# Cross-attention queries by Strassen's scheme, in half groups of four heads

## The chip, the cores and the metric

One core of one Trainium2 chip runs the whole program. The metric is the device time of one execution in microseconds (us), smaller is better. TensorE multiplies matrices (PE in the profile, PEld for its weight loads), VectorE (DVE), ScalarE (ACT) and GpSimd (POOL) work on elements, and SyncE (SP) issues the DMA transfers.

## The reference, cut to what matters

One decoder layer in float32: self-attention, cross-attention, feed-forward. The change is in the cross-attention. Its latents are the normalised x (8 batches, 128 rows, 512 features):

```python
q = (latents @ Wq).reshape(b, q_len, N_KV_HEADS, N_GROUPS, HEAD_DIM)   # 32 heads of 128
k = (hidden_states @ Wk).reshape(b, kv_len, N_KV_HEADS, HEAD_DIM)      # 4 heads, 256 keys
v = (hidden_states @ Wv).reshape(b, kv_len, N_KV_HEADS, HEAD_DIM)
scores = jnp.einsum('bqhgd,bkhd->bhgqk', q, k) * scale
attn = jax.nn.softmax(scores.astype(jnp.float32), axis=-1).astype(q.dtype)
out = jnp.einsum('bhgqk,bkhd->bqhgd', attn, v)
return out.reshape(b, q_len, N_HEADS * HEAD_DIM) @ Wo
```

## The kernel before, in words

Every float32 operand is kept as a rounded high part and a low part that holds the rest (names with h and l). ScalarE writes the high part, VectorE or GpSimd the low part, and each product is three matmuls: high by high, high by low, low by high (split3, lines 222 to 224). So each unit of matrix work costs three matmuls on TensorE.

The latents stand transposed in XTh and XTl: four blocks of 128 features (kc) by 1024 columns, 128 of them for each batch. The 32 query heads are taken in four groups of eight that share a key head. A group is 32 steps; step k treats two heads of one batch. On TensorE a step has these blocks, in this order:

- S: the scores of step k + 2 (scores_b), 6 matmuls of 256 columns;
- V: in every even step, probabilities times values of the last four heads (outputs), 6 matmuls of 512 columns;
- T: four transposes of the probabilities of step k;
- O: a quarter of the output product of the batch before (out_piece, two heads), 6 matmuls of 512 columns, summed in bank 7 over the eight heads of the group, then added to x_res by VectorE (residual);
- Q: half of a query block (queries, one head by half of the batches), 6 matmuls of 512 columns; a block takes 12 matmuls in bank 6 over two steps. There are 64 blocks: 8 ahead of the first step and 56 in the steps, to step 15 of the last group.

Beside it, VectorE takes the maxima of S, ScalarE the exponentials, VectorE the reciprocals of the sums and GpSimd multiplies (norm), two steps ahead of T. After T, ScalarE writes PTh and VectorE PTl; V waits for them. Weights come through four raw slots: SP loads a slot when GpSimd has taken the low part of what was in it. Keys and values of a batch (KV, 512 KB) have three slots, each refilled when the V blocks of the batch in it are done; the next batch is loaded two batches ahead, 32 loads in all. SP does all this in the order of its program: a load whose wait isn't met holds up those behind it.

The order of work on each engine is written out by hand, with semaphores between the engines. After the last group come the expert product, the last O and V blocks, and the feed-forward part in four rounds (pair).

Of the kernel before, what the change touches and what calls it, by code (L numbers as in the profile page):

```python
# [33 lines left out]
P = 128  # L34
# [13 lines left out]
XG = XH // XKV  # L48
KEYS = 2 * P
# [14 lines left out]
def decoder_layer(nc, x, ctx, s_wq, s_wk, s_wv, s_wo, x_wq, x_wk, x_wv, x_wo, gate_w, up_w, down_w,  # L64
                  fc1_w, fc2_w, expert_w, gamma, beta, rope, out):
    with ExitStack() as stack:
# [96 lines left out]
        WOh = sb("WOh", "WO", 0, [XG, D], F32R)  # L163
        WOl = sb("WOl", "WO", 16, [XG, D], F32R)


        Qh = sb("Qh", "Q", 0, [4, 2, 4, P], F32R)
        Ql = sb("Ql", "Q", 16, [4, 2, 4, P], F32R)
        Oh = sb("Oh", "O", 0, [2, XG, P], F32R)
        Ol = sb("Ol", "O", 8, [2, XG, P], F32R)  # L170
# [22 lines left out]
        EXTh = sb("EXTh", "KV", 8, [LC, LAT], F32R)  # L193
        EXTl = sb("EXTl", "KV", 10, [LC, LAT], F32R)
# [60 lines left out]

        ld_ex, c_a_e, c_v_e = sem("ld_ex"), sem("c_a_e"), sem("c_v_e")
# [13 lines left out]
        WPG = 2 * XG  # L270
# [17 lines left out]
        def chunk_steps(last):  # L288

            steps = [((0, 0, 1, 2, 3, 4, 5, 5)[h], "wo", h) for h in range(XG)]  # L290
            if not last:
                steps += [(8 + 2 * h, "wq", h) for h in range(XG)]
            else:
                steps += [(6 + 2 * i, "ffn", i) for i in range(NUP)]
                steps += [(22 + i - NUP, "ffn", i) for i in range(NUP, NUP + NFC)]
                steps += [((17, 19, 21, 26, 27, 28, 29, 30)[c], "ffn", NUP + NFC + c) for c in range(IC)]
            return sorted(steps, key=lambda step: step[0])
# [8 lines left out]
        def targets(kind, i):  # L306
            if kind == "wo":
                return WOh[:, i, :], WOl[:, i, :]
            if kind == "wq":
                return WQh[:, i, :, :], WQl[:, i, :, :]  # L310
            return ffn_chunks[i][1:]
# [4 lines left out]
        def ffn_ready(i):  # L316

            order = [n for n, (_, kind, j) in enumerate(chunk_steps(True)) if kind == "ffn" and j == i]
            return W0 + WPG * (XKV - 1) + order[0] + 1

# [4 lines left out]
        def query_cells(t, head, half):  # L325

            i, h = head // 2, head % 2
            return t[:, :, h, i, :] if half else t[:, i, h, :, :]

        def query_cell(t, head, b):  # L330
            i, h = head // 2, head % 2
            return t[:, b % HALF, h, i, :] if b // HALF else t[:, i, h, b % HALF, :]
        LN3_STEPS = (8, 12)
        EX_STEP = 26
# [30 lines left out]
        def _(sp):  # L365
# [48 lines left out]
            for b in range(3):  # L414
                sp.dma_start(f32(KV[:, b, :]), kv_scratch[0, b]).then_inc(b_kv[b], 16)
# [12 lines left out]
            def first_loads(g):  # L428

                for n in range(4):  # L430
                    src = wo_src(g, n)
                    sp.wait_ge(b_g_w, W0 + WPG * g + n - 3)
                    sp.dma_start(raw[:, n, :], src).then_inc(b_ld[n], 16)

            first_loads(0)
# [4 lines left out]
            def group(g, last):  # L440
                kv_loads = [(4 * (b - 3) + 4, g, b) for b in range(3, NB)]
                if not last:
                    kv_loads += [(24, g + 1, 2), (28, g + 1, 0), (32, g + 1, 1)]
                w_loads = [(max(step - 2, 0), kind, i) for step, kind, i in chunk_steps(last)]
                for k in range(DUOS):
                    for n, (step, kind, i) in enumerate(w_loads):
                        if step == k and n >= 4:

                            sp.wait_ge(b_g_w, W0 + WPG * g + n - 3)
# [39 lines left out]
        def _(gp):  # L489
# [83 lines left out]
            def norm(g, k):  # L573
                gp.wait_ge(b_v_rec, DUOS * g + k + 1)
# [33 lines left out]
            for g in range(XKV):  # L608
                group(g, g == XKV - 1)
# [1225 lines left out]
```

## Time and profile before

| | |
|---|---|
| median of 3 runs | 1024.8 us (1023.59 to 1025.76) |
| the profiled execution, own time | 1024.6 us |
| its span, first to last instruction | 1022.9 us |
| PE, PEld busy | 99%, 83% |
| DVE, ACT, POOL busy | 59%, 51%, 38% |
| granted TensorE clock, mean | 1.000 |
| DMA, mean | 67 GB/s |

Busy shares are of the span. Matmuls overlap in the pipeline, so the mean duration of a matmul is longer than the distance from one to the next; what a block costs is read as the distance between the starts of two blocks in the timeline.

### The profile page before, as it was taken

The numbers are of one execution on the slowest core, as the hardware profiler recorded it, in microseconds if no ns is written. First come the engines' busy times: TensorE is split into PE (matmuls) and PEld (weight loads), VectorE is DVE, ScalarE is ACT, GpSimd is POOL, SyncE is SP. The second block draws the span as 40 slices with busy tenths as digits, with TensorE's granted clock in tenths as the row PEclk, the third lists the DMA queues.
The fourth block names the chain that finished last, engine by engine and source line by source line (L and its number), as shares of the span: only waits on it lengthen the run. The fifth ranks groups of instructions, "written<-read, shape, count | busy, mean of one in ns | idle before, by whom it ended". The sixth has DMA issues, their size and how long they took to land.

```text
span 1022.9 us, 15694 instructions
## 1 busy us (share of the span) xinstructions
PE 1012.8 (99%) x5624; PEld 850.4 (83%) x5624; DVE 603.5 (59%) x1176; ACT 522.6 (51%) x1591; POOL 387.9 (38%) x369
## 2 busy tenths in 40 slices
PE   8999999999999999999999999999999999999997
PEld 7777777777888888888888888888888888899996
DVE  6888888878434545454545445444545556545654
ACT  5766667666524655445545445545436457522211
POOL 3645544544142533324433324333226447412110
PEclk9999999999999999999999999999999999999999
DMA  9410111104552221111211203112112133100000
GB/s 329 126 38 18 29 42 42 42 21 141 169 153 72 65 83 43 63 51 53 83 42 54 82 21 93 42 42 72 63 41 84 42 102 98 29 21 21 21 21 21
DMA packets 70248, 68.38 MB, mean 67 GB/s; under 512 B 4000, under 2 KB 54176, under 8 KB 70176
## 3 DMA queue, kind: packets, MB, share of 16 engines
q1 hardware_dynamic: 70176, 67.43, 21.3%
q8 instruction: 43, 0.70, 0.3%
q14 instruction: 29, 0.24, 0.1%
HBM read 48.55 MB, written 18.87 MB: 66 GB/s over the span
## 4 chain that ended last, share of the span: by engine, by line
PE 94%; DVE 2%; DMA 1%; ACT 1%; issue 1%; SPq 1%; POOL 0%; DVEq 0%; POOLq 0%
PE bank L222 27%; PE bank L224 26%; PE bank L223 26%; PE bank L1019 5%; PE bank L759 3%; PE bank L721 1%; PE bank L725 1%; DMA rawO<-in_L_attn_Wo_dram 1%; PE bank L728 1%; PE bank L731 1%; DVE Kbdl L1482 0%; PE bank L674 0%; PE bank L934 0%; PE bank L686 0%; PE bank L667 0%
## 5 line engine op out<-in xcount | busy, mean ns | idle before, releaser
L576 POOL TENSOR_TENSOR Pb<-Pb,b_rec 128x512 f32<-128x512 f32 x128 | 133.8, 1046 | 346.3 <-DVE b_rec L1634 346.3
L1629 DVE TENSOR_REDUCE b_nb<-bank 128x2 f32<-128x512 f32 x128 | 87.9, 687 | 85.6 <-PE bank L224 85.5
L1119 ACT ACTIVATE PTh<-bank 128x512 fp32r<-128x512 f32 x128 | 76.3, 596 | 117.3 <-PE bank L1019 117.3
L1262 ACT ACTIVATE Pb<-bank,b_nb 128x256 f32<-128x256 f32 x256 | 119.0, 477 | 4.5 <-DVE b_nb L1629 4.5
L1176 ACT ACTIVATE Pa<-bank,a_nb 128x128 f32<-128x128 f32 x256 | 90.8, 369 | 45.5 <-DVE a_nb L1507 44.8
L222 PE MATMUL bank<-WOh,Oh 128*128 128x512 f32 x256 | 110.6, 432 | 0.2
L538 POOL TENSOR_TENSOR Pa<-Pa,a_rec 128x512 f32<-128x512 f32 x64 | 68.3, 1067 | 102.0 <-DVE a_rec L1513 101.4
L1383 DVE TENSOR_TENSOR PTl<-bank,PTh 128x512 fp32r<-128x512 f32 x128 | 87.9, 687 | 25.4 <-ACT PTh L1119 25.4
L222 PE MATMUL bank<-XTh,WQh 128*128 128x512 f32 x256 | 101.6, 397 | 0.0
L224 PE MATMUL bank<-WOh,Ol 128*128 128x512 f32 x256 | 100.9, 394 | 0.0
L223 PE MATMUL bank<-WOl,Oh 128*128 128x512 f32 x256 | 100.4, 392 | 0.0
L224 PE MATMUL bank<-XTh,WQl 128*128 128x512 f32 x256 | 100.0, 390 | 0.0
L223 PE MATMUL bank<-XTl,WQh 128*128 128x512 f32 x256 | 99.7, 390 | 0.0
L1638 DVE SCALAR_TENSOR_TENSOR Ql<-bank,Qh 128x512 fp32r<-128x512 f32 x64 | 44.2, 692 | 80.4 <-ACT Qh L1269 80.4
L1119 ACT ACTIVATE Oh<-bank 128x512 fp32r<-128x512 f32 x64 | 38.3, 599 | 88.8 <-PE bank L224 88.8
L1383 DVE TENSOR_TENSOR Ol<-bank,Oh 128x512 fp32r<-128x512 f32 x64 | 44.3, 692 | 59.9 <-ACT Oh L1119 59.9
L1019 PE MATMUL bank<-ident,Pb 128*128 128x128 f32 x512 | 76.8, 272 | 0.0
L224 PE MATMUL bank<-KV,Ql 128*128 128x256 f32 x256 | 72.4, 283 | 0.0
L223 PE MATMUL bank<-KV,Qh 128*128 128x256 f32 x256 | 72.3, 283 | 0.0
L1269 ACT ACTIVATE Qh<-bank 128x512 fp32r<-128x512 f32 x64 | 38.3, 600 | 66.5 <-PE bank L224 66.5
L222 PE MATMUL bank<-KV,Qh 128*128 128x256 f32 x256 | 71.9, 281 | 0.0
L1019 PEld LDWEIGHTS bank<-ident,Pb 128*128 128x128 f32 x512 | 61.3, 140 | 8.4
(230 smaller groups left out, 2648.4 us busy)
## 6 DMA issues: line engine op xcount, KB each, us to landing
kv_scratch<-KVst SPq DMA_DIRECT2D x64, 256.0 KB, 3.0
KV<-kv_scratch SPq DMA_DIRECT2D x32, 512.0 KB, 3.4
raw<-in_L_xattn_Wo_dram SPq DMA_DIRECT2D x32, 256.0 KB, 3.4
raw<-in_L_xattn_Wq_dram SPq DMA_DIRECT2D x24, 256.0 KB, 4.2
cx<-in_ctx_dram SPq DMA_DIRECT2D x8, 256.0 KB, 9.9
raw_first<-in_L_xattn_Wq_dram SPq DMA_DIRECT2D x8, 256.0 KB, 4.5
raw<-in_L_ffn_up_w_dram SPq DMA_DIRECT2D x8, 256.0 KB, 4.0
raw<-in_L_ffn_down_w_dram SPq DMA_DIRECT2D x8, 256.0 KB, 2.8
```

Of the source, the lines that this page charges most:

```text
L222: pe.matmul(dst, lh, rh, start=start, stop=False)
L223: pe.matmul(dst, lh, rl, start=False, stop=False)
L224: return pe.matmul(dst, ll, rh, start=False, stop=stop)
L538: gp.tensor_tensor(pj, pj, a_rec[:, SG * j:SG * j + SG].unsqueeze(2).to_broadcast([P, SG, P]), ALU.mult).then_inc(g_norm, 1)
L576: gp.tensor_tensor(pk, pk, b_rec[:, k % 4, :].unsqueeze(2).to_broadcast([P, 2, KEYS]), ALU.mult).then_inc(b_g_norm, 1)
L1019: op = pe.transpose(bank[3 + k % 2][:, c * KEYS + h * P:c * KEYS + (h + 1) * P], Pb[:, k % 4, h, c * P:(c + 1) * P], ident[:])
L1119: return act.activation(dst, src, ACT.Copy)
L1176: op = act.activation(Pa[:, j % PS, c * P:(c + 1) * P], bank[2 + j % 3][:, c * P:(c + 1) * P], ACT.Exp, bias=a_nb[:, h:h + 1], scale=1.0, ...
L1262: op = act.activation(Pb[:, k % 4, h, :], bank[k % 3][:, h * KEYS:(h + 1) * KEYS], ACT.Exp, bias=b_nb[:, k % 4, h:h + 1], scale=1.0, accum ...
L1383: return dve.tensor_tensor(dst, src, f32(hi_part), ALU.subtract)
L1629: dve.tensor_reduce(b_nb[:, k % 4, :], bank[k % 3][:].rearrange("p (h k) -> p h k", h=2), AX.X, ALU.max, negate=True).then_inc(b_v_nb, 1)
L1638: dve.scalar_tensor_tensor(out=query_cells(Ql, head, half), in0=bank[bk][:].rearrange("p (b n) -> p b n", b=HALF), scalar=X_SCALE, in1=f32 ...
```

## The change

The groups become half groups of four heads (HG): eight units u of 16 steps (PER), 64 visits v to a batch of two steps each (VISITS), 128 steps in one loop (STEPS), as many as before. S, V, T and O keep their number and size. What differs:

- Query blocks of units 0 and 1 are made as before (8 ahead of the first step, 8 in steps 0 to 15). The other 48 come in 12 groups n of four blocks: two heads by both halves of the batches. Each group is a 2 by 2 product of blocks, made by Strassen's scheme in the Winograd form with seven products of half the depth. Product p of group n is made in step 16 + 8n + p; the eighth step of each group has no Q block. A product is 2 kc by 3, 6 matmuls of 512 columns, so 42 matmuls take the place of 48.
- The left operands of the products (OPh, OPl) are made of two raw weight chunks, 6 steps ahead: four sums on GpSimd of 256 elements a partition (operand_sums), seven high parts on ScalarE (operand_hi) and seven low parts on GpSimd (operand_lo).
- The right operands need sums of latents T1 to T4, made once in steps 2 to 16: eight sums, each two GpSimd instructions and one on VectorE, then high and low part.
- After products 0, 1 and 2 ScalarE copies the running sum in bank 6 to U (partial), and the next product is added on in the same bank. Product 3 completes a block as before. After products 4, 5 and 6 VectorE adds the bank to a U (query_sum), ScalarE writes the high part (query_hi) and GpSimd the low part (query_lo).
- bank 7 is summed over four heads, so x_res is added to 64 times (residual), not 32. The output weights have six places (WOS).
- Keys and values are loaded for each visit, 64 times 512 KB, into three slots. The load for visit v waits for the V block of visit v - 3 (in step 2v - 4), and S needs it at the start of step 2v - 2. In each step of SP it is issued ahead of the weight chunks.
- At the end TensorE runs the expert product, the last V, two O blocks, the transposes of turn_x3, and the last two O blocks.

```diff
-DUOS = NB * XG // 2
-PB = XG // 2
-QUADS = DUOS // 2
-BLOCK = NB // 2 * PB
-QB = PB // 2
+GROUPS = XH // HG
+VISITS = GROUPS * NB
+STEPS = 2 * VISITS
+PER = 2 * NB
...
+        OPh = sb("OPh", "WQ", 0, [7, 2, P], F32R)
...
+        S1 = sb("S1", "WQ", 7, [2 * P])
+        S2 = sb("S2", "WQ", 23, [2 * P])
+        U = [sb("U1", "WQ", 12, [D]), sb("U2", "WQ", 14, [D]), sb("U3", "WQ", 28, [D])]
+        T1h = sb("T1h", "O", 8, [2, D], F32R)
...
+        T2h = sb("T2h", "WO", 24, [2, D], F32R)
...
+        T4h = sb("T4h", "WQ", 8, [2, D], F32R)
...
+        Tf = sb("Tf", "F", 0, [2, D])
+        Qh = sb("Qh", "Q", 0, [2, 2, 2, 2, 2, P], F32R)
...
+        UNIT0, UNITS_Q, PRODUCTS = PER, 2 * (GROUPS - 2), 7
...
+        CHUNKS = [((0, 0, 1, 2)[h], "wo", (0, h), h) for h in range(HG)]
+        CHUNKS += [((PER * (u - 1) + 7, PER * (u - 1) + 10, PER * u + 3, PER * u + 3)[h], "wo", (u, h), 2 + h % 2)
+                   for u in range(1, GROUPS) for h in range(HG)]
+        CHUNKS += [(step, "ffn", i, slot) for i, (step, slot) in enumerate(UP_STEPS + FC_STEPS + DN_STEPS)]
...
+        PAIRS = [(8 * n + 10, "pair", n, slot) for n in range(UNITS_Q) for slot in range(2)]
...
+        def chunk_load_step(step, kind, i, slot):
+            if kind == "pair":
+                return 8 * i + 6 if i else 2
+            ahead = chunk_ahead(kind, i, slot)
+            if ahead and ahead[1] == "pair":
+                return max(step - 3, ahead[0] + 5)
+            return max(step - 3, ahead[0] + 1 if ahead else 0)
...
+        SUMS = ((0, 0, 0), (1, 1, 2), (0, 1, 1))
+        B = [[(XTh[:, 2 * k:2 * k + 2, c * D:(c + 1) * D], XTl[:, 2 * k:2 * k + 2, c * D:(c + 1) * D])
+              for c in range(2)] for k in range(2)]
+        T1, T2, T3, T4 = (T1h, T1l), (T2h, T2l), B[0][1], (T4h, T4l)
+        LATENT_SUMS = [(dst, a, b, kc) for dst, a, b in ((T1, B[0][1], B[0][0]), (T2, B[1][1], T1),
+                                                         (T4, B[1][0], T2), (T3, B[1][1], B[0][1]))
+                       for kc in range(2)]
+        T_STEPS = (2, 3, 5, 6, 8, 9, 13, 14)
+        T_SPLIT = (4, 5, 7, 8, 10, 11, 15, 16)
+        RIGHT = (B[0][0], T2, T3, T4, B[1][0], T1, B[1][1])
...
+        def pair_step(k):
+            return [(n, k - 8 * n - 10) for n in range(UNITS_Q) if 0 <= k - 8 * n - 10 < PRODUCTS]
+        def product_step(k):
+            n, p = (k - UNIT0) // 8, (k - UNIT0) % 8
+            return (n, p) if 0 <= n < UNITS_Q and p < PRODUCTS else (None, None)
+        def products(n, p):
+            return BLOCKS + PRODUCTS * n + p + 1
...
+            def load_chunk(kind, i, slot):
+                ahead = chunk_ahead(kind, i, slot)
+                if ahead and ahead[1] == "pair":
+                    sp.wait_ge(b_g_s, PRODUCTS * ahead[2] + 5)
+                elif ahead:
+                    sp.wait_ge(b_g_w, split_count(*ahead[1:3]))
+                if kind == "pair":
...
+                    src = wq_src(u // 2, HG * (u % 2) + head + slot)
...
+                else:
+                    src = wo_src(i[0] // 2, HG * (i[0] % 2) + i[1]) if kind == "wo" else ffn_chunks[i][0]
+                    dst = raw_view(slot, targets(kind, i)[0])
+                sp.dma_start(dst, src).then_inc(b_ld[slot], 16)
+            for h in range(HG):
+                load_chunk("wo", (0, h), h)
             for n in range(U_E0 + 2, NU):
                 store_unit(n)
             stored(NU)
-            def group(g, last):
-                kv_loads = [(4 * (b - 3) + 4, g, b) for b in range(3, NB)]
-                if not last:
-                    kv_loads += [(24, g + 1, 2), (28, g + 1, 0), (32, g + 1, 1)]
-                w_loads = [(max(step - 2, 0), kind, i) for step, kind, i in chunk_steps(last)]
-                for k in range(DUOS):
-                    for n, (step, kind, i) in enumerate(w_loads):
-                        if step == k and n >= 4:
-                            sp.wait_ge(b_g_w, W0 + WPG * g + n - 3)
-                            dst = targets(kind, i)[0]
-                            src = (wo_src(g, i) if kind == "wo" else wq_src(g + 1, i) if kind == "wq"
-                                   else ffn_chunks[i][0])
-                            sp.dma_start(raw_view(n % 4, dst), src).then_inc(b_ld[n % 4], 16)
-                    if k == 26 and not last:
-                        first_loads(g + 1)
-                    for done, gg, b in kv_loads:
-                        if done == k + 1:
-                            sp.wait_ge(b_pe_pv, QUADS * g + done // 2)
-                            sp.dma_start(f32(KV[:, b % 3, :]), kv_scratch[gg, b]).then_inc(b_kv[b % 3], 16)
-            for g in range(XKV):
-                group(g, g == XKV - 1)
-            sp.wait_ge(b_pe_wo, PB * NB * XKV + 1)
+            for k in range(STEPS):
+                if k % 2 and k // 2 + 3 < VISITS:
+                    v = k // 2 + 3
+                    sp.wait_ge(b_pe_pv, v - 2)
+                    sp.dma_start(f32(KV[:, kv_slot(v), :]),
+                                 kv_scratch[v // NB // 2, v % NB]).then_inc(b_kv[kv_slot(v)], 16)
+                for step, kind, i, slot in sorted(CHUNKS + PAIRS, key=lambda c: chunk_load_step(*c)):
+                    if chunk_load_step(step, kind, i, slot) == k and (kind, i[0] if kind == "wo" else 1) != ("wo", 0):
+                        load_chunk(kind, i, slot)
...
+            def operand_sums(n, p):
+                if p == 0:
+                    if n == 0:
+                        gp.wait_ge(b_pe_q, NB)
+                    for slot in range(2):
+                        gp.wait_ge(b_ld[slot], load_count("pair", n, slot))
+                    gp.tensor_tensor(S1[:], raw_half(1, 0), raw_half(1, 1), ALU.add).then_inc(b_g_f, 1)
+                    gp.wait_ge(b_g_f, 4 * n + 1)
+                    gp.tensor_tensor(S2[:], S1[:], raw_half(0, 0), ALU.subtract).then_inc(b_g_f, 1)
+                if p == 1:
+                    gp.wait_ge(b_g_f, 4 * n + 2)
+                    gp.tensor_tensor(raw_half(1, 0), raw_half(0, 0), raw_half(1, 0), ALU.subtract).then_inc(b_g_f, 1)
+                if p == 2:
+                    gp.wait_ge(b_g_s, PRODUCTS * n + 2)
+                    gp.tensor_tensor(S2[:], raw_half(0, 1), S2[:], ALU.subtract).then_inc(b_g_f, 1)
+            def operand_lo(n, p):
+                src = (raw_half(0, 0), S2[:], raw_half(1, 0), raw_half(1, 1), raw_half(0, 1), S1[:], S2[:])[p]
+                gp.wait_ge(b_a_s, PRODUCTS * n + p + 1)
+                gp.tensor_tensor(OPl[:, p, :, :].rearrange("p k n -> p (k n)"), src,
+                                 f32(OPh[:, p, :, :].rearrange("p k n -> p (k n)")), ALU.subtract).then_inc(b_g_s, 1)
+            def query_lo(n, s):
+                u, head = unit_blocks(n)
+                h, half, at_u = SUMS[s]
+                gp.wait_ge(b_a_q, BLOCKS + 4 * n + s + 2)
+                gp.tensor_tensor(query_cells(Ql, u, head + h, half), four(U[at_u][:]),
+                                 f32(query_cells(Qh, u, head + h, half)), ALU.subtract).then_inc(b_g_q, 1)
...
+            def latent_sum(c):
+                dst, a, b, kc = LATENT_SUMS[c]
+                if c == 0:
+                    gp.wait_ge(v_htl, NB)
+                else:
+                    gp.wait_ge(t_v, (0, 0, 1, 2, 3, 4, 5, 6)[c])
+                gp.tensor_tensor(Tf[:, c % 2, :], f32(a[0][:, kc, :]), f32(b[0][:, kc, :]), ALU.subtract).then_inc(t_g, 1)
+                gp.wait_ge(t_g, 2 * c + 1)
+                gp.tensor_tensor(Tf[:, c % 2, :], Tf[:, c % 2, :], f32(a[1][:, kc, :]), ALU.add).then_inc(t_g, 1)
+            for k in range(STEPS):
+                if k + 2 < STEPS:
+                    norm(k + 2)
+                n, p = product_step(k - 1)
+                if n is not None and p >= 4:
+                    query_lo(n, p - 4)
+                for n, p in pair_step(k):
+                    operand_sums(n, p)
+                if k - 1 in LN3_STEPS:
+                    inv_std(LN3_STEPS.index(k - 1) + 1)
+                for step, kind, i, slot in CHUNKS:
+                    if step == k:
+                        hi, lo = targets(kind, i)
+                        lo_part(raw_view(slot, lo), split_count(kind, i), lo, hi)
+                for n, p in pair_step(k):
+                    operand_lo(n, p)
+                if k in T_STEPS:
+                    latent_sum(T_STEPS.index(k))
...
+            def query_product(n, p):
+                pe.wait_ge(b_g_s, PRODUCTS * n + p + 1)
+                if n == 0 and p in (1, 2):
+                    pe.wait_ge(t_v, (6, 8)[p - 1])
+                if p == 0:
+                    pe.wait_ge(b_v_q, BLOCKS + 4 * n)
+                elif p < 4:
+                    pe.wait_ge(b_a_u, 3 * n + p)
+                else:
+                    pe.wait_ge(b_v_q, BLOCKS + 4 * n + p - 3)
+                rh, rl = RIGHT[p]
+                for kc in range(2):
+                    for n_op, (lhs, rhs) in enumerate(((OPh, rh), (OPh, rl), (OPl, rh))):
+                        op = pe.matmul(bank[6][:], lhs[:, p, kc, :], rhs[:, kc, :],
+                                       start=p in (0, 4, 5) and kc == 0 and n_op == 0, stop=kc == 1 and n_op == 2,
+                                       skip_group_check=p not in (0, 4, 5))
+                op.then_inc(b_pe_q, 1)
...
+            for k in range(STEPS):
+                if k + 2 < STEPS:
+                    if k:
+                        pe.wait_ge(b_a_exp, k)
+                    scores_b(k + 2)
+                if k == 0:
+                    pe.wait_ge(b_v_q, 6)
+                    first_queries(7)
+                if k and k % 2 == 0:
+                    outputs(k // 2 - 1)
+                pe.wait_ge(b_g_norm, k + 1)
+                pe.wait_ge(b_v_pt, k + 1)
+                for c in range(2):
+                    for h in range(2):
+                        op = pe.transpose(bank[3 + k % 2][:, c * KEYS + h * P:c * KEYS + (h + 1) * P],
+                                          Pb[:, k % 4, h, c * P:(c + 1) * P], ident[:])
+                op.then_inc(b_pe_pt, 1)
+                if k >= 4:
+                    out_piece(k // 2 - 2, k % 2)
+                if k < UNIT0:
+                    head, half = block_order(k // 2)
+                    if k % 2 == 0:
+                        pe.wait_ge(b_v_q, NB + k // 2 - (1 if k == 0 else 0))
+                    op = queries(W0, HG + head, half, 6, ((0, 1), (2, 3))[k % 2])
+                    if k == UNIT0 - 2:
+                        op.then_inc(b_pe_b12, 1)
+                n, p = product_step(k)
+                if n is not None:
+                    query_product(n, p)
+                if k == EX_STEP:
+                    turn_expert()
+            expert_product()
+            outputs(VISITS - 1)
+            for i in range(2):
+                out_piece(VISITS - 2, i)
+            turn_x3(0)
+            for i in range(2):
+                out_piece(VISITS - 1, i)
...
+            def operand_hi(n, p):
+                src = (raw[:, 0, 0:2 * P], S2[:], raw[:, 1, 0:2 * P], raw[:, 1, 2 * P:4 * P], raw[:, 0, 2 * P:4 * P],
+                       S1[:], S2[:])[p]
+                if p in (0, 3, 4):
+                    slot = int(p == 3)
+                    act.wait_ge(b_ld[slot], load_count("pair", n, slot))
+                else:
+                    act.wait_ge(b_g_f, 4 * n + {1: 2, 2: 3, 5: 1, 6: 4}[p])
+                act.wait_ge(b_pe_q, products(n - 1, p) if n else NB)
+                hi(OPh[:, p, :, :].rearrange("p k n -> p (k n)"), src).then_inc(b_a_s, 1)
+            def partial(n, p):
+                act.wait_ge(b_pe_q, products(n, p))
+                if n:
+                    act.wait_ge(b_g_q, 3 * n - 3 + (1, 3, 2)[p])
+                act.activation(U[p][:], bank[6][:], ACT.Copy, scale=X_SCALE).then_inc(b_a_u, 1)
+            def query_hi(n, s):
+                u, head = unit_blocks(n)
+                h, half, at_u = SUMS[s]
+                act.wait_ge(b_v_q, BLOCKS + 4 * n + s + 2)
+                hi(query_cells(Qh, u, head + h, half), four(U[at_u][:])).then_inc(b_a_q, 1)
...
+            def query_sum(n, s):
+                at_u = SUMS[s][2]
+                dve.wait_ge(b_pe_q, products(n, s + 4))
+                dve.wait_ge(b_a_u, 3 * n + at_u + 1)
+                dve.scalar_tensor_tensor(out=U[at_u][:], in0=bank[6][:], scalar=X_SCALE, in1=U[at_u][:],
+                                         op0=ALU.mult, op1=ALU.add).then_inc(b_v_q, 1)
+            def latent_sum(c):
+                _, _, b, kc = LATENT_SUMS[c]
+                dve.wait_ge(t_g, 2 * c + 2)
+                dve.tensor_tensor(Tf[:, c % 2, :], Tf[:, c % 2, :], f32(b[1][:, kc, :]), ALU.subtract).then_inc(t_vf, 1)
+            def latent_lo(c):
+                dst, _, _, kc = LATENT_SUMS[c]
+                dve.wait_ge(t_a, c + 1)
+                lo(dst[1][:, kc, :], Tf[:, c % 2, :], dst[0][:, kc, :]).then_inc(t_v, 1)
+            def residual(v):
+                dve.wait_ge(b_pe_wo, 2 * v + 3)
+                dve.tensor_tensor(x_res[:, v % NB, :], x_res[:, v % NB, :], bank[7][:], ALU.add).then_inc(b_v_x, 1)
```

## Rows read from the trace of the kernel before

**Rows 1.** The page: span, and busy time of each engine

```profile
span 1022.9 us, 15694 instructions
...
PE 1012.8 (99%) x5624; PEld 850.4 (83%) x5624; DVE 603.5 (59%) x1176; ACT 522.6 (51%) x1591; POOL 387.9 (38%) x369
```

**Rows 2.** Waits of TensorE: engine and line, who released it, us, times, longest

```profile
PE bank L849 <- DVE ident_r L1386: 2.1, 1, 2.1
```

**Rows 3.** Stretches: busy us of each engine, granted clock, DMA share, GB/s

```profile
325.00:473.00 148.00, 147.95 (x801) 126.30 (x800) 72.77 (x135) 74.15 (x209) 53.31 (x48) 1.00 0.19 58
...
834.00:896.00 62.00, 61.97 (x350) 53.12 (x349) 35.05 (x65) 37.98 (x103) 34.38 (x30) 1.00 0.24 73
```

**Rows 4.** Timeline of TensorE, a step with Q: start us, duration us, line

```profile
602.84 0.39 PE L222 MATMUL bank<-XTh,WQh 128*128 128x512 f32 x1
...
604.20 0.28 PE L222 MATMUL bank<-KV,Qh 128*128 128x256 f32 x1
...
604.91 0.40 PE L222 MATMUL bank<-PTh,KV 128*128 128x512 f32 x1
...
606.30 0.60 PE L1019 MATMUL bank<-ident,Pb 128*128 128x128 f32 x4
606.66 0.48 PE L222 MATMUL bank<-WOh,Oh 128*128 128x512 f32 x1
...
608.14 0.39 PE L222 MATMUL bank<-XTh,WQh 128*128 128x512 f32 x1
```

**Rows 5.** Timeline of TensorE in the last group's steps without Q

```profile
846.22 0.60 PE L1019 MATMUL bank<-ident,Pb 128*128 128x128 f32 x4
...
848.05 0.28 PE L222 MATMUL bank<-KV,Qh 128*128 128x256 f32 x1
...
848.76 0.40 PE L222 MATMUL bank<-PTh,KV 128*128 128x512 f32 x1
...
850.14 0.60 PE L1019 MATMUL bank<-ident,Pb 128*128 128x128 f32 x4
```

**Rows 6.** Instructions by form: all, count, busy us, mean ns, idle before

```profile
L576 POOL TENSOR_TENSOR Pb<-Pb,b_rec 128x512 f32<-128x512 f32 x128 | 133.8, 1046 | 346.3 <-DVE b_rec L1634 346.3
L1262 ACT ACTIVATE Pb<-bank,b_nb 128x256 f32<-128x256 f32 x256 | 119.0, 477 | 4.5 <-DVE b_nb L1629 4.5
...
L1638 DVE SCALAR_TENSOR_TENSOR Ql<-bank,Qh 128x512 fp32r<-128x512 f32 x64 | 44.2, 692 | 80.4 <-ACT Qh L1269 80.4
...
L529 POOL TENSOR_TENSOR WOl<-raw,WOh 128x512 fp32r<-128x512 f32 x32 | 41.1, 1294 | 4.5 <-ACT WOh L1119 4.5
...
L1269 ACT ACTIVATE Qh<-bank 128x512 fp32r<-128x512 f32 x64 | 38.3, 600 | 66.5 <-PE bank L224 66.5
...
L1646 DVE TENSOR_TENSOR x_res<-x_res,bank 128x512 f32<-128x512 f32 x32 | 21.5, 671 | 11.8 <-PE bank L224 11.8
```

**Rows 7.** ScalarE, VectorE and GpSimd in one of those steps, timeline

```profile
846.86 0.60 ACT L1119 ACTIVATE PTh<-bank 128x512 fp32r<-128x512 f32 x1 [0.46 <-PE bank L1019]
...
847.49 0.69 DVE L1383 TENSOR_TENSOR PTl<-bank,PTh 128x512 fp32r<-128x512 f32 x1 [0.38 <-ACT PTh L1119]
...
848.65 1.04 POOL L576 TENSOR_TENSOR Pb<-Pb,b_rec 128x512 f32<-128x512 f32 x1 [0.20 <-DVE b_rec L1634]
```

**Rows 8.** Keys and values: SP's issues, and from issue to landing

```profile
L460 SPq DMA_DIRECT2D KV<-kv_scratch x29: 326/327/339, 339.0 to 850.3; - x29
...
DMA to landing us min/median/max: 3.1/3.4/4.1
```

**Rows 9.** Timeline of SP's DMA issues near step 20 of the last group

```profile
850.33 0.33 SPq L460 DMA_DIRECT2D KV<-kv_scratch  x1
```

**Rows 10.** The page: DMA issues, count, KB each, median us to landing

```profile
raw<-in_L_xattn_Wq_dram SPq DMA_DIRECT2D x24, 256.0 KB, 4.2
```

**Rows 11.** VectorE, two instructions of one kind and shape, by form

```profile
L1577 DVE TENSOR_SCALAR xn<-x_res,mv,rstd 128x512 f32<-128x512 f32 x8 | 10.3, 1284 | 0.7 <-POOL rstd L554 0.7
...
L1428 DVE TENSOR_SCALAR xn<-x_res,mv,rstd 128x512 f32<-128x512 f32 x8 | 4.2, 524 | 0.7 <-POOL rstd L503 0.7
```

More of the change, by code:

```diff
@@ L585, in _ @@
                 first_wq_lo(h)
-            norm(0, 0)
-            norm(0, 1)
-            def group(g, last):
-                chunks = chunk_steps(last)
-                def split_weights(k):
-                    for n, (step, kind, i) in enumerate(chunks):
-                        if step == k:
-                            hi, lo = targets(kind, i)
-                            lo_part(raw_view(n % 4, lo), W0 + WPG * g + n + 1, lo, hi)
-                for k in range(DUOS):
-                    if k + 2 < DUOS:
-                        norm(g, k + 2)
-                    elif not last:
-                        norm(g + 1, k + 2 - DUOS)
-                    if last and k - 1 in LN3_STEPS:
-                        inv_std(LN3_STEPS.index(k - 1) + 1)
-                    split_weights(k)
-                split_weights(DUOS)
@@ L608, in _, with raw_half @@
-            for g in range(XKV):
-                group(g, g == XKV - 1)
+            norm(0)
+            norm(1)
+            def raw_half(slot, k):
+                return raw[:, slot, 2 * P * k:2 * P * (k + 1)]
+            def operand_sums(n, p):
[13 more added lines that the diff above has]
+                    gp.tensor_tensor(S2[:], raw_half(0, 1), S2[:], ALU.subtract).then_inc(b_g_f, 1)
@@ L1044, in _ @@
-            for g in range(XKV):
-                group(g, g == XKV - 1)
-            pe.wait_ge(b_g_w, ffn_ready(NUP + NFC - 1))
+            for k in range(STEPS):
[29 more added lines that the diff above has]
+                    turn_expert()
@@ L1252, in _, with probs_b @@
                 batch(b, b == NB - 1)
[L1255 to L1260 removed]
+            def probs_b(k):
+                act.wait_ge(b_v_nb, k + 1)
                 for h in range(2):
@@ L1349, in _, with weight @@
-            for g in range(XKV):
-                group(g, g == XKV - 1)
+                hi(Oh[:, v % 2, :, :], bank[5][:].rearrange("p (h n) -> p h n", h=HG)).then_inc(b_a_o, 1)
+            def weight(step, kind, i, slot):
+                if kind == "wo":
+                    u, h = i
+                    if h < 2:
+                        act.wait_ge(b_pe_wo, 2 * NB * (u - 1) + 1 if u > 1 else 1)
+                    else:
+                        act.wait_ge(b_pe_wo, 2 * NB * u if u else 1)
+                elif i < NUP:
+                    if i >= 6:
+                        act.wait_ge(b_g_q, 3 * UNITS_Q - 7 + i)
+                    else:
+                        act.wait_ge(b_pe_q, products(UNITS_Q - 1, (1, 3, 5, 6, 3, 3)[i]))
+                elif i < NUP + NFC:
+                    act.wait_ge(b_pe_s, STEPS - 8)
+                else:
+                    act.wait_ge(b_pe_q, products(UNITS_Q - 1, PRODUCTS - 1))
+                act.wait_ge(b_ld[slot], load_count(kind, i, slot))
+                dst = targets(kind, i)[0]
+                hi(dst, raw_view(slot, dst)).then_inc(b_a_w, 1)
@@ L1353, in x3_hi @@
+            act.wait_ge(c_pe_e, 2)
+            for lc, bk in enumerate((6, 1)):
+                hi(F2h[:, lc, :], bank[bk][:]).then_inc(c_a_e, 1)
+            outputs(VISITS - 1)
             def x3_hi(c):
@@ L1734, in pair @@
+            for lc, bk in enumerate((6, 1)):
+                dve.wait_ge(c_a_e, 2 + lc)
+                lo(F2l[:, lc, :], bank[bk][:], F2h[:, lc, :]).then_inc(c_v_e, 1)
+            outputs(VISITS - 1)
+            residual(VISITS - 2)
+            x3_lo(0)
+            residual(VISITS - 1)
             def pair(c, last):
```

451 lines of the change are left out of this document (215 added, 236 removed).

## The prediction

> **What bounds the kernel now.** I read the page first: TensorE is busy 1012.8 of 1022.9 us, the other engines 59%, 51% and 38% [rows 1]. A busy share can hide small stalls, so next come the waits of TensorE: the longest is 2.1 us, at the warm-up, and nothing in the cross-attention is listed [rows 2]. The table by stretches says the same of the part that changes: 147.95 of 148.00 us busy in the first group and 61.97 of 62.00 us in the last steps, which have no Q, with a granted clock of 1.00 in both, the 2.4 GHz level [rows 3]. So TensorE's program is the time, in the steps with Q and in those without it. A matmul that goes is worth its distance to the next one, provided no other engine or load becomes late.
>
> The timeline gives that distance. From the start of Q to the start of S are 1.36 us for 6 matmuls, 0.227 us each; S takes 0.71 us, V 1.39 us, T 0.36 us, O 1.48 us with its first matmul behind T [rows 4]. The mean durations of 0.39 us that the records show would overstate the gain by two thirds. Without Q, T and O together take 1.83 us and V 1.38 us [rows 5].
>
> **The change part by part.** *Matmuls.* 12 groups have 42 matmuls in place of 48: 12 Q blocks fewer, 72 matmuls, 12 x 1.36 = 16.3 us. The count of S, V, T and O is the same, and so is their shape; the seven products load as many weights a matmul as before. Sums that go on in bank 6 without a fresh start are the same instruction as the second and later matmuls of a block today, so I price them alike. The bounds from the rows: 0.227 us, and at most the 0.23 us spacing of V (1.39 / 6), which gives 16.7 us.
>
> A rule weighed here: the Trainium skill (TensorE: Matmul & The Clock Gate, Back-to-back issue gap) gives 512/2.4 + 2.5, about 216 ns, from matmul to matmul. By it the 72 would be worth an estimated 15.6 us. The row's distance is 5% longer and includes the weight load of each, so the row decides.
>
> *Work on the other engines.* Eight steps with Q take 4 x (3.20 + 0.71 + 3.20 + 0.71 + 1.39) = 36.8 us, where 3.20 is T + O + Q; with one Q gone 35.5 us. GpSimd has 8 norms at 1.05 us and per group 7 operand low parts, 4 sums, 3 query low parts and 2 output weights. No row has 256 elements on GpSimd; the bounds are nothing and the 1.29 us of 512 elements [rows 6]. Even all 16 at 1.29 make 29.1 us, and I take 22 (0.65 us for a half, by the halved length). ScalarE was busy 74.15 in 148 us, 18.5 in eight steps [rows 3]; the 7 operands at 0.48 to 0.60 us replace 2 weights, and 3 more copies of 0.60 us come [rows 6], at most 4.8 us more, 23.3 of 35.5. VectorE goes from 18.2 to 19.5 us by two more residuals of 0.67 us; query_sum costs what the low part of Q does, 0.69 us [rows 6]. Nobody comes near 35.5 us, so this is hidden behind TensorE; uncovered, it would be 9 or 10 us in each group.
>
> *The new waits.* After products 0 to 2 ScalarE waits for Q at the end of its step, then copies for 0.60 us. Behind it in its queue are Oh or PTh of the next step, which can't start before S and V or S and T. The next product needs the copy S + T + O = 2.55 us later at the earliest, so 1.7 us remain with some 0.2 us of signalling. Product 4 waits for ScalarE and VectorE in turn, 0.60 + 0.69 us, in an even step of 3.94 us to Q. Operands are made six steps ahead. query_hi and query_lo have the next step for it, and S reads them two steps or more later. I cost these at nothing.
>
> *The steps without Q.* Here T to V is the shortest: O and S, then V needs PTl. The last group has this case now. T starts at 846.22 [rows 5], PTl runs 847.49 to 848.18 [rows 7], V starts at 848.76: 0.58 us to spare. In the 12 new ones, ScalarE and VectorE come out of a full step with 3.9 us or more for it, so they are free at T. Cost nothing; the bound is a wait of one ScalarE or VectorE instruction, 0.6 us in each, 7 us.
>
> *Keys and values.* 64 loads in place of 32, and the slack shrinks. Today a slot is refilled several steps ahead. Now a load may start at the end of V in an even step and must be there for S two steps on. That window is T, O, Q, S, T, O, Q = 7.1 us in most steps, 5.75 us where the second step has no Q (12 loads), and 1.83 + 0.71 + 1.83 = 4.37 us for the first load and the last six [rows 4, 5]. Issue to landing took 3.1 to 4.1 us, median 3.4 [rows 8], and SP issues 0.19 us after V's end (850.33 [rows 9] against T at 850.14 [rows 5]). So 3.6 us are needed, 4.3 at worst, and the 4.37 us just hold. What can spoil it is other traffic or SP being held. Pair loads (two of 256 KB, 4.2 us [rows 10]) are let go by the fifth operand low part. That is some 5.4 us after T of an even step: norm starts 2.43 us after T [rows 5, 7] and takes 1.05 us, a query low part 1.29 and the operand 0.65. The next KV load follows 2.6 us later (after 3.20 + 0.71 + 1.83 + 0.71 + 1.39 + 0.19 = 8.0 us), in a window of 7.1 us: hidden. In the tail, three weight loads that wait for GpSimd's chunks of step 115 go out close ahead of the load for visit 61, window 4.37 us: I take 0.5 us, and at most 1.0 (the spread of 3.1 to 4.1) for each of the seven short windows, 7 us, as the far bound. All 61 loads have to pass SP past weight loads; issuing them first in their step keeps those of the same step behind them.
>
> *Start and end.* GpSimd's latent sums come in pairs of at most 2.6 us, in steps 2 and 3 back to back with norm, where T to T is only 2.55 us (T, Q with 0.12 us more behind T, S) and 3.9 us (with V). GpSimd falls behind, and VectorE waits for it in steps 3 and 4, with the maxima, Ol and PTl queued behind that wait. The following V has about 1 us left. I take 0.2 us, at most 2. Near step 124 ScalarE has two weights and the expert matrix ahead of PTh of step 125; V of step 126 may be some 0.2 us late. At the end O of visit 63 waits for residual 62: 0.67 us plus signals against eight transposes, twice T's 0.36 us: 0.1 us. Group boundaries were without a gap and give nothing.
>
> **The sum.** -16.3 + 0.5 + 0.2 + 0.2 + 0.1 = -15.3 us. The profiled execution took 1024.6 us by its own time (span 1022.9), 0.2 us under the median of 1024.8, so 1009.3 from the profile and 1009.5 against the median. I say 1009.5.
>
> **Rivals.** *Keys and values late in the short windows, and weights between them.* Speaks for it: 4.37 us against 3.3 to 4.3. Against: the loads are small against what the DMA moves, share 0.19 to 0.24 [rows 3]. 2 to 7 us back: 1011 to 1016.
>
> *Another engine sets the pace around the products.* A chain of ScalarE, VectorE and GpSimd through U, or PTl in the steps without Q. For: three engines in turn on one buffer, 0.58 us of slack. Against: 1.7 us in the product steps. With 0.6 us lost in each of the 12 groups 7 us go, with all the 1.36 us in each everything: 1013 to 1024.8. In the last case the change does less matrix work and no less time.
>
> *VectorE and GpSimd block each other.* One kind of VectorE instruction took 1.28 us in one place and 0.52 us in another, same shape, with GpSimd active beside it [rows 11]. If the eight latent sums of VectorE do so and nothing covers them, they and the queue behind lose up to 1.29 us each: 10.3 us, 1020. I give the full price hardly anything, since 1 us or more of slack covers most. The Trainium skill (SBUF — State Buffer, Who interferes with whom) says that a VectorE instruction with two SBUF inputs contends with a GpSimd instruction that reads SBUF; by it these eight are the ones to look at, and the slow row fits but does not show the partner.
>
> *Slower: keys and values late at every visit.* Should the doubled traffic make a load take longer than its window, each of some 61 visits stalls TensorE. It decides at 16.3 / 61 = 0.27 us a visit, a landing above about 7.2 us in the wide windows; at 8 us it costs some 60 us, 1070. Today's worst is 4.1 us [rows 8]. 4%.
>
> **How the numbers follow.** The forecast, 1008 to 1011, has 70%; the first rival 13%, the second 8% (2 of them with no gain left), the third 5%, the slower one 4%. The range that keeps 80% and takes in the bounds for the short windows is 1008.0 to 1014.5. About 0.2% (2 us) is what a measurement of this kernel can tell from no change: faster 0.94, within it 0.02, slower 0.04.
>
> **What the profile after would show.** Q matmuls 192 + 504 instead of 768; distance of six of them still 1.36 us; TensorE's waits nearly empty, at most 1 or 2 us, most of it in steps 112 to 127; KV x64 landing at 3 to 5 us; TensorE's busy time 16 us less. Stalls of S on KV in the wide windows, a product that waits on U, or V on PTl once in eight steps would make it wrong, and so would a spacing above 0.23 us in the products.

## The result, and the profile after

The changed kernel took 1009.29 us, median of 4 runs (1008.21 to 1010.24), against 1024.57 us before (4 runs): ratio 0.985, 95% interval 0.9833 to 0.9867. It is 15.3 us faster, as forecast in sign and size (1009.5); by the interval the gain lies between 13.6 and 17.1 us. The profiled execution took 1010.24 us by its own time, span 1008.5.

The page: against the kernel before [rows 1] TensorE's busy time falls by 16.5 us and its matmuls by 72, and the other engines are busier. Keys and values are loaded 64 times.

```profile
span 1008.5 us, 16102 instructions
...
PE 996.3 (99%) x5552; PEld 837.9 (83%) x5552; DVE 641.1 (64%) x1224; ACT 558.6 (55%) x1695; POOL 519.5 (52%) x529
...
KV<-kv_scratch SPq DMA_DIRECT2D x64, 512.0 KB, 3.3
```

The waits of TensorE, longest first (us in all, times, longest):

```profile
PE bank L993 <- DVE ident_r L1600: 2.1, 1, 2.1
PE bank L782 <- DMA rawKV<-in_L_attn_Wv_dram: 1.9, 1, 1.9
PE bank L237 <- DVE PTl L1597: 1.1, 2, 0.9
```

The 1.9 us for rawKV are at the program's start, where the change doesn't reach. The waits of that line differ from execution to execution: in the three control profiles of the same kernel below they add up to 1.0 to 1.5 us, and other releasers are named too. So I compare stretches that begin at the first transpose T of the cross-attention and end at the first feed-forward matmul; 4 profiles of the changed kernel (this one and three controls) gave 555.11 to 555.46 us. First after, then before:

```profile
327.38:882.52 555.14, 553.90 (x3039) 474.68 (x3037) 329.90 (x593) 333.96 (x934) 359.78 (x364) 1.00 0.28 93
```

```profile
325.84:896.86 571.02, 570.70 (x3112) 488.02 (x3110) 293.01 (x545) 297.53 (x830) 227.61 (x204) 1.00 0.20 61
```

That is 15.9 us less, 15.6 to 15.9 by the four profiles. VectorE has 36.9, ScalarE 36.4 and GpSimd 132.2 us more to do in it, and TensorE waited 1.2 us in all. The clock granted is 1.00, the 2.4 GHz level, in both.

A product that starts a sum (product 4, step 60), then one that goes on with a sum (product 6, step 62) and the step without Q that follows it, on TensorE's timeline; before, see [rows 4, 5]:

```profile
593.70 0.40 PE L1143 MATMUL bank<-XTh,OPh 128*128 128x512 f32 x1
...
595.09 0.28 PE L237 MATMUL bank<-KV,Qh 128*128 128x256 f32 x1
...
602.93 0.39 PE L1143 MATMUL bank<-XTh,OPh 128*128 128x512 f32 x1
...
604.29 0.28 PE L237 MATMUL bank<-KV,Qh 128*128 128x256 f32 x1
...
605.00 0.60 PE L1187 MATMUL bank<-ident,Pb 128*128 128x128 f32 x4
605.36 0.48 PE L237 MATMUL bank<-WOh,Oh 128*128 128x512 f32 x1
...
606.83 0.28 PE L237 MATMUL bank<-KV,Qh 128*128 128x256 f32 x1
...
607.54 0.40 PE L237 MATMUL bank<-PTh,KV 128*128 128x512 f32 x1
...
608.92 0.27 PE L1187 MATMUL bank<-ident,Pb 128*128 128x128 f32 x1
```

The six matmuls that go on with a sum take 1.36 us (602.93 to 604.29), as a block of Q did before, and the six that start one some 1.38 (593.70 to 595.09). All 84 products took 1.36 to 1.38 us, so going on with a sum costs nothing more. From T at 605.00, O and S are followed by V at 607.54 after 2.54 us, nothing waits: ScalarE and VectorE had PTl ready. The three places where TensorE waits longer than in the kernel before are step 6, step 126 and the last O blocks.

### The profile page after: what moved, and what is told of

The parts are those of the page before. It is cut to its first block, busy times and chain, and to the rows that moved or that the text cites. A ratio compares the mean times of both kernels' runs of the same rounds, so it can differ in the third digit from the quotient of the medians.

```text
span 1008.5 us, 16102 instructions
## 1 busy us (share of the span) xinstructions
PE 996.3 (99%) x5552; PEld 837.9 (83%) x5552; DVE 641.1 (64%) x1224; ACT 558.6 (55%) x1695; POOL 519.5 (52%) x529
## 4 chain that ended last, share of the span: by engine, by line
PE 93%; DVE 3%; ACT 1%; issue 1%; DMA 1%; POOL 1%; DVEq 0%; POOLq 0%; SPq 0%; ACTq 0%
PE bank L237 23%; PE bank L239 22%; PE bank L238 22%; PE bank L1143 11%; PE bank L1187 5%; PE bank L903 3%; PE bank L864 1%; PE bank L868 1%; PE bank L871 1%; PE bank L874 1%; DMA rawKV<-in_L_attn_Wv_dram 1%; DVE Kbdl L1696 0%; ACT Pb L1424 0%; PE bank L817 0%; PE bank L810 0%
## 5 line engine op out<-in xcount | busy, mean ns | idle before, releaser
L1285 ACT ACTIVATE PTah<-bank 128x512 fp32r<-128x512 f32 x72 | 43.4, 602 | 32.5 <-PE bank L903 24.4
L679 POOL TENSOR_TENSOR rstd<-var_eps,half 128x1 f32<-128x1 f32 x16 | 12.3, 767 | 92.0 <-DVE var_eps L1633 92.0
L1597 DVE TENSOR_TENSOR PTal<-bank,PTah 128x512 fp32r<-128x512 f32 (+1 forms) x88 | 50.3, 586 | 11.4 <-ACT PTah L1285 10.8
L239 PEld LDWEIGHTS bank<-WOh,Ol 128*128 128x128 f32 x256 | 48.0, 188 | 11.3
L238 PEld LDWEIGHTS bank<-WOl,Oh 128*128 128x128 f32 x256 | 48.6, 190 | 6.0
```

The source lines that it names most:

```text
L238: pe.matmul(dst, lh, rl, start=False, stop=False)
L239: return pe.matmul(dst, ll, rh, start=False, stop=stop)
L1285: return act.activation(dst, src, ACT.Copy)
L1597: return dve.tensor_tensor(dst, src, f32(hi_part), ALU.subtract)
```

## The experiments

Each is an edit of the changed kernel. Where the stretch is given it is that of the profile, as above.

**1. Fill the steps without Q.** Twelve blocks of 6 matmuls of 512 columns, identity by identity, that serve nothing.

```diff
+                if UNIT0 <= k < 112 and (k - UNIT0) % 8 == 7:
+                    pe.wait_ge(b_v_q, BLOCKS + 4 * ((k - UNIT0) // 8) + 4)
+                    for _ in range(6):
+                        pe.matmul(bank[6][:].rearrange("p (c k) -> p c k", c=SG), ident_r[:],
+                                  ident_r[:].unsqueeze(1).to_broadcast([P, SG, P]), start=True, stop=True)
```

> In the 12 steps that have no Q block TensorE gets 6 more matmuls of 512 columns (identity by identity, into bank 6 once VectorE has read it, so they add nothing to the result). TensorE then has as many matmuls as the kernel before. If the gain is the 72 matmuls at 0.227 us and nothing else, it goes back: +12 x 1.36 = 16.4 us, 1025.7 us, within 1 us of the kernel before. Rival: half groups and the new order of work gain or cost something of their own; then it stands clearly off the kernel before, by the 0.6 us of the group boundaries and the 1 to 2 us of new waits or more.

Measured: 1025.07 us, ratio to before 1.0007 (0.9998 to 1.0017). The stretch:

```profile
325.56:897.28 571.72, 570.51 (x3111) 488.23 (x3109) 330.81 (x593) 334.04 (x934) 360.01 (x364) 1.00 0.28 90
```

It is 16.5 us above the changed kernel's 555.2 (the middle of its four profiles), 1.37 us a block, and 0.7 us above the kernel before. The theory held and the rival didn't: the gain is the 72 matmuls; the rest of the change, all of it together, costs 0.7 us net.

**2. Latent sums later.** `T_STEPS = (4, 5, 7, 8, 10, 11, 13, 14)` in place of (2, 3, 5, 6, 8, 9, 13, 14), T_SPLIT to match.

> The latent sums start at step 4 in place of 2 (steps 4, 5, 7, 8, 10, 11, 13, 14) and no longer stand in the two short steps. Theory, GpSimd falls behind there and VectorE's queue waits for it: the 0.4 us wait of V on PTl in step 6 is gone, total 0.4 to 0.5 us less. Rival, the sums hold VectorE and GpSimd against each other wherever they stand: a wait of V or S shows up elsewhere in steps 4 to 16.

Measured: one run of 1010.23 us, stretch 556.6, 1.4 us longer. The wait in step 6 is gone, but V of step 14 now starts 1.98 us after the last matmul of S, where 0.12 us is the usual distance: 1.9 us late. VectorE's timeline there: it waits for GpSimd until 382.61, its latent sum takes 1.51 us, then come the maxima and only then PTl, which V needs:

```profile
382.61 1.51 DVE L1871 TENSOR_TENSOR Tf<-Tf,T2l 128x512 f32<-128x512 f32 x1 [1.18 <-POOL Tf L733]
384.04 0.68 DVE L1843 TENSOR_REDUCE b_nb<-bank 128x2 f32<-128x512 f32 x1
384.64 0.68 DVE L1597 TENSOR_TENSOR PTl<-bank,PTh 128x512 fp32r<-128x512 f32 x1
```

The rival was right: the wait moved, and grew. The sums now stand in steps 10 and 11, where GpSimd also has the operand sums and a weight; that this is why it grew is argued, not tested.

**3. The third term of the sums on GpSimd.**

```diff
                 gp.tensor_tensor(Tf[:, c % 2, :], Tf[:, c % 2, :], f32(a[1][:, kc, :]), ALU.add).then_inc(t_g, 1)
+                gp.wait_ge(t_g, 2 * c + 2)
+                gp.tensor_tensor(Tf[:, c % 2, :], Tf[:, c % 2, :], f32(b[1][:, kc, :]), ALU.subtract).then_inc(t_vf, 1)
...
-                    if T_STEPS[c] == k - 1:
-                        latent_sum(c)
```

> The third term of each latent sum goes from VectorE to GpSimd, at the same steps. Theory, V in step 6 waits because VectorE's queue stands behind its latent sum (waits for GpSimd, then 1.5 us in place of 0.7): the 0.4 us goes although GpSimd has 1.3 us more for each sum. Rival, GpSimd is what is late (norm behind the sums): the wait grows by about 1.3 us, or moves to T.

Measured: one run of 1008.77 us, stretch 554.7, 0.5 us less, and no wait in steps 4 to 16. GpSimd had room for a third instruction; it was VectorE's queue, as the theory had it. The span was 1006.2 us, so 2.6 us of the run lie outside it, see the last section.

**4. The expert matrix earlier.** `EX_STEP = 119` in place of 124.

> The expert matrix is turned in step 119, not 124. Theory, the 0.9 to 1.0 us wait of V on PTl in step 126 comes from ScalarE having two down weights and the expert matrix ahead of PTh of step 125, and VectorE the low part of the expert matrix and the maxima ahead of PTl: this wait goes, 1.0 us less, and step 119 has slack for the work. Rival, the two weights alone are enough to make PTh late: 0.3 us or more of it stays.

Measured: 1007.74 us, one run, stretch 554.45, 0.8 us less. From the start of O to V, in step 126, it took 1.78 us and not 2.53. The usual is 1.48, so 0.3 us are left, the limit that the rival had named. Of these, 0.2 us stand at the same place in the kernel before, and 0.1 us goes when one of the two weights is moved as well (experiment 8). So most of the wait was the expert matrix, as the theory had it, and 0.1 us the weights.

**5. Experiments 2 and 4 together.**

> Latent sums from step 4 and the expert matrix in step 119 together. If the waits in steps 6 and 126 are what they cost in the profile, 0.5 + 1.0 = 1.5 us less than the changed kernel, 1007.8 us, ratio to before 0.9836. Rival, the time is given back at the next wait: no difference from the changed kernel.

Measured: 1009.80 us, ratio 0.9856 (0.984 to 0.9873), against the control's 1009.67. The stretch is 555.9, just the sum of both: 1.4 us longer by experiment 2, 0.8 shorter by experiment 4. The wait in step 14 takes back more than step 126 brings. The rival was right. The changed kernel once more, as the control of experiments 5 to 7:

> The changed kernel again, as the control of this call: 1009.3 us, ratio 0.985.

It took 1009.67 us, ratio 0.985 (0.9834 to 0.9867).

**6. Keys and values 1.84 us later.** `sp.wait_ge(b_pe_wo, k - 1)` ahead of each of these loads from step 3 on.

> Each load of keys and values also waits for the O block of its step, 0.36 + 1.48 = 1.84 us later. Theory, a load needs 3.6 us from V's end (0.2 + 3.1 to 4.1, and some signalling), so the windows have slack of 3.5, 2.1 and 0.8 us: the wide ones (5.3 us left) and those with a step without Q (3.9 left) still hold, the last six (2.5 left) stall S by 1.1 us each, some 6 us in all, 1015 to 1017. Rival, loads collide with weights so that many already need the whole window: stalls in the 12 windows of 3.9 us too, 1020 or more. Second rival, loads land much faster than the records say: no change.

Measured: 1017.45 us, ratio 0.9927 (0.991 to 0.9944), 7.8 us over the control. The waits of TensorE:

```profile
PE bank L237 <- DMA KV<-kv_scratch: 6.0, 5, 1.5
...
PE bank L237 <- ACT Pb L1426: 1.1, 1, 1.1
PE bank L237 <- DVE PTl L1599: 1.0, 2, 0.7
```

Six waits are those of S at the start of steps 114 to 124, 1.1 to 1.7 us each. Five are put down to KV. The sixth, put down to Pb, is of the same kind: Pb was written by 840.92, the keys landed at 841.81 and S started at 841.90. The theory held, with waits somewhat longer than its 1.1 us, so that the time lies 0.45 us above its 1015 to 1017; neither rival did, since S stalled, but in no window of 3.9 or 5.3 us. With 2.53 us of window left, a load needs 3.6 to 4.2 us from the moment that it is let go to S (2.53 us and the wait). So the last windows of the changed kernel, 4.37 us, should have 0.2 to 0.8 us to spare. Its own profile agrees: there these six loads landed 0.4 to 1.0 us ahead of their S, and in this experiment S started 0.1 us after the landing. The change holds there narrowly.

**7. Weights ahead of keys and values** within each step of SP.

> In each step of SP the weight chunks are issued ahead of the load of keys and values, not behind it. It matters where an odd step has both (about 11 steps: 7, 23, 39, ... and 103 to 121). Theory, SP gets held by the weights' wait or adds up to 1 us of transfer, which the 7.1 us windows hide and the 4.37 us ones do not: 0 to 3 us slower, all of it as waits of S on KV in steps 112 to 122. Rival, the order is what makes the doubled loads affordable: 5 us or more slower.

Measured: 1008.83 us, ratio 0.9847 (0.9826 to 0.9867); control 1009.67. Stretch 555.1, no wait for KV. That is the low end of the theory, and the rival's 5 us are excluded: the order of issue is worth nothing that can be measured here.

**8. A better version?** Experiments 3 and 4, and the down weight `(124, 0)` in step 125; then the same without experiment 3; each beside a control.

> The third term of the latent sums on GpSimd, the expert matrix in step 119, and one down weight of step 124 in step 125. Theory: the waits in steps 6, 124 and 126 are gone and nothing takes their place, since none of the three moves work into the steps 10 to 15, where the shifted sums of the earlier combination stalled: from the first transpose of the cross-attention to the first feed-forward product 553.4 us, 1.9 us less than the changed kernel; total 1007.6 us. Rival: the time is given back at another wait, as in that combination: 555 us and no difference in the total.

> The changed kernel as the control of this call: 1009.5 us, stretch 555.3 us.

> The expert matrix in step 119 and one down weight of step 124 in step 125, with the latent sums as in the changed kernel. Theory: the waits in steps 124 and 126 go as in the run with all three, 0.9 to 1.2 us of the stretch, and the time outside the span is 1.7 us again, since the 2.5 to 2.8 us came with the third term on GpSimd: span and total both 1.0 us under the control. Rival: the time outside the span varies with any edit, or the time is given back, and the total stays within 0.3 us of the control.

> The changed kernel as the control of this call: 1009.0 us, stretch 555.3 us, 1.7 us outside the span.

| | total us | ratio to before | median span | stretch |
|---|---|---|---|---|
| all three | 1008.55 | 0.9841 (0.9827 to 0.9854) | 1005.9 | 553.8 |
| its control | 1008.75 | 0.9844 (0.9831 to 0.9858) | 1007.0 | 555.1 |
| without experiment 3 | 1008.23 | 0.9841 (0.9827 to 0.9854) | 1006.3 | 554.6 |
| its control | 1008.86 | 0.9845 (0.9831 to 0.9858) | 1007.1 | 555.2 |

Inside the span the three edits bring 1.1 us, in the stretch 1.3 where 1.9 were expected. The two that are left without experiment 3 bring 0.8 us in the span and 0.6 in the stretch, where 1.0 and 0.9 to 1.2 were expected. For all three, TensorE's list of waits no longer has one of the cross-attention (SQl is made at 11 to 14 us):

```profile
PE bank L995 <- DVE ident_r L1602: 2.1, 1, 2.1
PE bank L784 <- DMA rawKV<-in_L_attn_Wv_dram: 0.7, 1, 0.7
PE bank L784 <- ACT rawOg L1396: 0.6, 1, 0.6
PE bank L237 <- DVE SQl L1599: 0.2, 1, 0.2
```

The total moves by 0.2 and 0.6 us, less than the 1 us and more that was expected of both, and the intervals don't tell it from nothing. No version was shown to beat the changed kernel.

## Why the prediction was right, by its own steps

**The matmuls** (-16.3 us): 16.5 by experiment 1, and the distance of 0.227 us held in sums that go on in the bank. This term made the result. The prediction also weighed 216 ns from the Trainium skill (TensorE: Matmul & The Clock Gate, Back-to-back issue gap). That section gives them for a matmul by itself, and about 131 ns for a stream of weight loads and matmuls, which the prediction left out; by these the 72 would be worth an estimated 9.4 us. The traces agree with neither figure: 227 ns by the rows, 229 by experiment 1.

**Work on other engines hidden**: right. GpSimd's half-length instructions took 0.74 us where I had 0.65, query low parts 1.29:

```profile
L720 POOL TENSOR_TENSOR Ql<-U,Qh 128x512 fp32r<-128x512 f32 x36 | 46.4, 1289 | 0.0
...
L712 POOL TENSOR_TENSOR OPl<-raw,OPh 128x256 fp32r<-128x256 f32 x48 | 35.5, 739 | 0.9 <-ACT OPh L1285 0.9
```

Eight steps of the long middle, from T to T (length, then busy us of TensorE, its weight loads, VectorE, ScalarE and GpSimd):

```profile
502.55:538.02 35.47, 35.47 (x196) 30.44 (x195) 19.71 (x36) 20.61 (x59) 22.18 (x25) 1.00 0.24 82
```

I had 35.5 us, 19.5 for VectorE, at most 23.3 for ScalarE and 22 for GpSimd. The waits on U and the steps without Q cost nothing. The second rival, at 8%, did not occur anywhere.

**Keys and values** (+0.5 us): 0. No S waited for one. The spread of landings is wider than before [rows 8] and the median is not:

```profile
L556 SPq DMA_DIRECT2D KV<-kv_scratch x61: 319/326/339, 334.1 to 854.3; - x61
...
DMA to landing us min/median/max: 3.1/3.3/5.1
```

The five loads that took more than 3.8 us (3.9 to 5.1) are all in windows of 7.1 us and landed 1.9 us or more ahead of their S; in the last six windows they took 3.2 to 3.8 us. The first rival and the slower one did not come about, but experiment 6 shows how near the first one stood.

**The start** (+0.2 us): 0.4, V of step 6, which starts 0.51 us after the last matmul of S and not 0.12. TensorE, VectorE and GpSimd there:

```profile
348.02 0.28 PE L239 MATMUL bank<-KV,Ql 128*128 128x256 f32 x1
348.53 0.50 PE L237 MATMUL bank<-PTh,KV 128*128 128x512 f32 x1 [0.23 <-DVE PTl L1597]
```

```profile
341.25 1.51 DVE L1871 TENSOR_TENSOR Tf<-Tf,XTl 128x512 f32<-128x512 f32 x1 [1.50 <-POOL Tf L733]
342.68 0.68 DVE L1843 TENSOR_REDUCE b_nb<-bank 128x2 f32<-128x512 f32 x1
...
345.75 1.53 DVE L1871 TENSOR_TENSOR Tf<-Tf,XTl 128x512 f32<-128x512 f32 x1
347.19 0.68 DVE L1843 TENSOR_REDUCE b_nb<-bank 128x2 f32<-128x512 f32 x1
347.80 0.68 DVE L1597 TENSOR_TENSOR PTl<-bank,PTh 128x512 fp32r<-128x512 f32 x1
```

```profile
342.17 1.74 POOL L731 TENSOR_TENSOR Tf<-XTh 128x512 f32<-128x512 f32 x1
...
345.23 1.49 POOL L673 TENSOR_TENSOR Pb<-Pb,b_rec 128x512 f32<-128x512 f32 x1
```

VectorE's two latent sums take 1.5 us each, GpSimd's instructions beside them 1.74 and 1.49 in place of 1.29 and 1.04. In experiment 2's profile one of them has no GpSimd instruction beside it:

```profile
352.04 0.68 DVE L1871 TENSOR_TENSOR Tf<-Tf,XTl 128x512 f32<-128x512 f32 x1
```

So an overlap cost 0.8 us here, and up to 1.1 (the longest of the eight took 1.78 us), where the third rival had up to 1.29. It is that rival's mechanism, and nearly all of it was covered. The low parts of the latent sums, which read two tensors from SBUF as well, took 0.7 to 1.8 us; the prediction left them out. The Trainium skill (SBUF — State Buffer, Who interferes with whom) says that just this pair contends, a VectorE instruction with two SBUF inputs and a GpSimd one that reads SBUF; the trace agrees. The slow row of the prediction [rows 11] is not this pair, since it reads one tensor and two values a row. But its partner is in the trace of the kernel before: each of the eight starts 0.07 us behind the start of a GpSimd instruction, like the one below, and takes 1.25 us, the last one 1.50. Among the eight fast ones VectorE starts first in six: GpSimd's instruction begins 0.16 us behind it and is the one that gets longer, 1.25 us and not 1.04. The other two have none of that size beside them.

```profile
97.05 1.04 POOL L538 TENSOR_TENSOR Pa<-Pa,a_rec 128x512 f32<-128x512 f32 x1
97.12 1.25 DVE L1577 TENSOR_SCALAR xn<-x_res,mv,rstd 128x512 f32<-128x512 f32 x1
```

Experiment 3 took away the wait for GpSimd and the blocked instruction at once, so how the 0.4 us of the wait divide between them was not shown.

**Step 126** (+0.2 us): the wait was 0.9 us (O starts at 863.88 and V at 866.41, 2.53 us for a block of 1.48, less the 0.2 us that V is late at this place in the kernel before). I had counted what delays PTh on ScalarE; VectorE then has the expert matrix's low part and the maxima ahead of PTl:

```profile
864.47 0.69 DVE L1597 TENSOR_TENSOR EXTl<-bank,EXTh 128x512 fp32r<-128x512 f32 x1 [1.35 <-ACT EXTh L1285]
865.08 0.68 DVE L1843 TENSOR_REDUCE b_nb<-bank 128x2 f32<-128x512 f32 x1
865.68 0.68 DVE L1597 TENSOR_TENSOR PTl<-bank,PTh 128x512 fp32r<-128x512 f32 x1
```

V starts at 866.41. This term was mis-sized because I followed one queue of the two.

**The last O** (+0.1 us): 0.25, the eight transposes and the wait took 1.04 us, where the transposes took 0.79 in the kernel before (878.36 to 879.40, and 891.60 to 892.39).

**Group boundaries** ("without a gap"): wrong. The kernel before waited there for Oh and Ol, as its own chain of waits shows (start, us, what):

```profile
468.64 0.61 ACT Oh L1119
469.27 0.70 DVE Ol L1383
470.01 0.50 PE bank L222
```

The matmul of 469.57 is followed by the next only at 470.01, 0.44 us and not 0.23. At three boundaries (469.57, 617.30, 764.98) that is 0.6 us which the change takes away; I had read the busy time of whole stretches, where it hardly shows. It covers what the waits in step 126 and the last O cost above my terms.

Together: -16.5 + 0.4 + 0.9 + 0.25 - 0.6 = -15.6 us (15.55), where the stretches give 15.6 to 15.9 and the medians 15.3; I had -15.3. The term of the matmuls carried the forecast. That the sum of the small ones came out right to a few tenths is luck: I had keys and values 0.5 us too dear, the gain of the matmuls 0.2 us too small, the boundaries not at all, and the waits of the start, step 126 and the last O together 1.05 us too cheap.

## What to carry to other kernels

Where one engine is busy for the whole span, price a removed instruction by its distance to the next and not by its duration, and put the work into asking whether the others stay hidden. That takes following every queue up to the instruction that is waited for, VectorE's as well as ScalarE's. A small wait is mended by less work in the queue that is late. Another place for the work helps only where the queues have room: the expert matrix moved brought 0.8 us, the latent sums moved came back as a V that was 1.9 us late.

## What the hardware showed that I had not expected

The time outside the span was 1.66 to 1.83 us in 45 of the 47 runs of kernels that leave GpSimd's part as it is (2.71 us in one run of experiment 6 and in one of the version without experiment 3), but 2.45 to 2.77 us in all six runs with the third term on GpSimd (one of experiment 3, five of the version with all three edits). There it took back 0.9 of the 1.1 us that this version gained inside the span (1008.75 - 1007.0 = 1.75 us for the control, 1008.55 - 1005.9 = 2.65 us with the edits). Why the edit does this was not found.
